# Table casts and splits ahead of the preceding selection's copies in the head, and tile 14's last layer behind tile 15's first, in a gather, interaction and tower kernel

## The reference

```python
e = jnp.stack([tbl_0[ids[:, 0]], ..., tbl_31[ids[:, 31]]], axis=1)
dots = jnp.einsum('bnd,bmd->bnm', e, e)
z = dots[:, iu, ju]
h = jnp.concatenate([z, dense_ctx], axis=1)
h = jnp.maximum(h @ W_top1 + b_top1, 0.0)
h = jnp.maximum(h @ W_top2 + b_top2, 0.0)
y = h @ W_top3
```

## Time and profile before

| what | value |
|---|---|
| median of 3 runs | 585.84 us (584.89 to 585.88) |
| the profiled execution's own time | 583.17 us |
| its span | 581.1 us |
| TensorE matmuls busy | 503.9 us, 87% of the span |
| TensorE weight loads busy | 479.1 us, 82% |
| POOL busy | 419.8 us, 72% |
| VectorE busy | 360.5 us, 62% |
| ScalarE busy | 263.8 us, 45% |
| mean granted clock of TensorE | 0.977 |
| moved by DMA | 70.15 MB, mean 121 GB/s |

### The profile page before, as it was taken

One profiled execution on the slowest core, in us unless ns is written; L12 is line 12 of the kernel. 1 busy time (PEld: TensorE's weight loads), 2 busy tenths in 40 slices (PEclk: granted clock), 3 DMA queues, 4 the chain that ended last, 5 costly groups with the idle time before them and its releaser, 6 DMA issues.

```text
span 581.1 us, 16242 instructions
## 1 busy us (share of the span) xinstructions
PE 503.9 (87%) x7108; PEld 479.1 (82%) x7108; DVE 360.5 (62%) x747; ACT 263.8 (45%) x390; POOL 419.8 (72%) x440
## 2 busy tenths in 40 slices
PE   0266679999999999999999999999999999997786
PEld 0266679898989989898989899898989898996685
DVE  1334467676757577658667677657767675754543
ACT  0223255454546255444636345544645445533542
POOL 6777777777777777777777777777777777777710
PEclk9997799999999999999999999999999999998799
DMA  5999434444433444434443443444443443433310
GB/s 132 257 253 241 108 98 116 115 118 122 117 116 105 127 115 116 119 111 127 115 115 111 120 120 113 115 119 121 118 117 106 133 117 105 119 102 109 105 35 0
DMA packets 35595, 70.15 MB, mean 121 GB/s; under 512 B 13107, under 2 KB 18627, under 8 KB 35527
## 3 DMA queue, kind: packets, MB, share of 16 engines
q0 software_dynamic: 20832, 56.91, 35.1%
q1 hardware_dynamic: 14695, 12.22, 8.9%
HBM read 69.09 MB, written 0.01 MB: 119 GB/s over the span
## 4 chain that ended last, share of the span: by engine, by line
PE 40%; POOL 35%; issue 12%; DVE 5%; ACT 4%; DMA 2%; POOLq 0%; DVEq 0%
POOL rows L318 35%; PE sel_ps L416 15%; PE gram_ps L356 9%; PE tr_ps L332 7%; PE gram_ps L378 4%; DMA rows<-in_tbl,ids_sb 2%; PE gram_ps L388 2%; DVE sel_low L614 2%; ACT sel_high L769 1%; DVE onehot L631 1%; ACT emb_t L537 1%; DVE emb_t L537 1%; ACT emb_t L545 1%; PE gram_ps L396 1%; PE sel_ps L356 1%
## 5 line engine op out<-in xcount | busy, mean ns | idle before, releaser
L318 POOL DMA_INDIRECT rows<-in_tbl,ids_sb x434 | 419.1, 966 | 134.4 <-issue 129.8
L416 PE MATMUL sel_ps<-onehot,sel_high 125*128 125x256 f32 x624 | 164.6, 301 | 24.8 <-DVE sel_low L614 22.6
L537 ACT COPY emb_t<-tr_ps 128x512 f32<-128x512 f32 (+1 forms) x112 | 124.3, 1114 | 100.9 <-PE tr_ps L332 99.9
L416 PE MATMUL sel_ps<-onehot,sel_low 125*128 125x256 f32 x624 | 158.8, 291 | 0.0
L416 PEld LDWEIGHTS sel_ps<-onehot,sel_high 125*128 125x128 f32 x624 | 124.9, 200 | 30.4 <-DVE sel_low L614 23.8
L332 PE MATMUL tr_ps<-ident,rows 128*128 128x128 f32 x868 | 117.5, 279 | 33.2 <-DMA rows<-in_tbl,ids_sb 25.6
L537 DVE COPY emb_t<-tr_ps 128x512 f32<-128x512 f32 (+1 forms) x112 | 120.4, 1086 | 29.0 <-PE tr_ps L332 28.1
L332 PEld LDWEIGHTS tr_ps<-ident,rows 128*128 128x128 f32 x868 | 98.4, 143 | 38.7 <-issue 29.4
L356 PEld LDWEIGHTS gram_ps<-emb_t 128*64 128x64 f32 x3840 | 116.9, 139 | 15.3 <-issue 12.0
L356 PE MATMUL gram_ps<-emb_t 128*64 128x62 f32 x3840 | 121.8, 224 | 8.4 <-ACT emb_t L537 5.6
L416 PEld LDWEIGHTS sel_ps<-onehot,sel_low 125*128 125x128 f32 x624 | 125.1, 200 | 0.0
(11 more groups left out here) (48 smaller groups left out, 157.6 us busy)
## 6 DMA issues: line engine op xcount, KB each, us to landing
rows<-in_tbl,ids_sb POOLq DMA_INDIRECT x434
sel_raw<-in_tbl SPq DMA_DIRECT2D x5, 896.0 KB
sel_ids<-in_ids_by_field SPq DMA_DIRECT2D x35, 128.0 KB
w_sb<-in_W_top SPq DMA_DIRECT2D x1, 1024.0 KB, 22.8
sel_raw<-in_tbl SPq DMA_DIRECT2D x5, 104.0 KB
dots_t<-in_ids_by_field SPq DMA_DIRECT2D x4, 128.0 KB, 5.8
w_sb<-in_W_top SPq DMA_DIRECT2D x1, 512.0 KB, 27.0
ids_sb<-in_ids SPq DMA_DIRECT2D x1, 240.0 KB, 3.1
```

Source lines behind the costliest of these rows:

```text
L318: pool.indirect_dma_start(out=rows[:, slot, :], out_offset=None, in_=tables[f], in_offset=bass.IndirectOffsetOnAxis(ap=ids_sb[:, t, f:f + ...
L416: last = nc.tensor.matmul(sel_ps[j % 2][:, h, :], table[:, i, c, h * P:(h + 1) * P], onehot[:, c, :], start=(c == 0 and table is sel_high) ...
L537: copy(emb_t[t % PAIR][:, h, :, at[0]:at[-1] + 1].rearrange("p (g s) f -> p f s g", s=QUAD), tr_ps[h][g % 2][:, 0:len(at), :].rearrange("p ...
```

## The change

Three things change.

In the head, ScalarE casts the first two tables ahead of the first selection's copies, and each later table one place sooner than before. VectorE's splits move in the same way: splits 0 and 1 stand together behind quad 1, split 2 behind quad 2, split 3 behind quad 4, split 4 behind quad 5. The one-hots keep their places. TensorE's order in the head is the same.

In the tail, TensorE runs tile 14's layer 3 behind tile 15's layer 1 instead of ahead of tile 15's turn. VectorE runs tile 15's turn copy ahead of tile 14's layer 2 relu, and tile 14's y copy behind tile 15's layer 1 relu. ScalarE's order in the tail is the same.

The third part is bookkeeping: the number of gathered selected fields becomes a list with one entry for each pair of tiles, (1, 0, 0, 0, 0, 0, 0, 0), and the helpers that count jobs are written for such a list. The wait of a selection for its table is now asked for by every selection of pair 0 and by every selection of table 0, instead of by every selection of pairs 0 and 1.

```diff
-GATHERED_FIRST = 1
+GATHERED = (1, 0, 0, 0, 0, 0, 0, 0)
...
-        return n_rows + (GATHERED_FIRST if t < PAIR else 0)
+        return n_rows + GATHERED[t // PAIR]
...
-        p, at = (t + 1) // PAIR, range(0, EARLY) if t % PAIR else range(EARLY, n_sel)
-        if t == 0:
-            at = range(GATHERED_FIRST, n_sel)
-        return [(p, i) for i in at] if p < tiles // PAIR else []
+        p = (t + 1) // PAIR
+        if p >= tiles // PAIR:
+            return []
+        own = [(p, i) for i in range(GATHERED[p], n_sel)]
+        return own if t == 0 else own[:EARLY] if t % PAIR else own[EARLY:]
...
-                    if p < 2:
-                        pe.wait_ge(tables_split, (i - GATHERED_FIRST) % n_sel + 1)
+                    if i < GATHERED[0] or p == 0:
+                        pe.wait_ge(tables_split, table_place(i) + 1)
...
                 layer2(t - 1)
-                layer3(t - 1)
                 turn(t)
                 layer1(t)
+                layer3(t - 1)
                 layer2(t)
                 layer3(t)
...
                 turn_dots(t)
+                turn_copy(dve, 0, copy, t)
                 layer2_copy(dve, 0, bias_relu, t - 1)
+                layer1_copy(dve, 0, bias_relu, t)
                 y_copy(t - 1)
-                turn_copy(dve, 0, copy, t)
-                layer1_copy(dve, 0, bias_relu, t)
                 layer2_copy(dve, 0, bias_relu, t)
                 y_copy(t)
...
-            for g in range(quads):
-                emb_copy(dve, 0, copy, g)
-                if g in SELECT_AFTER:
-                    split_table(SELECT_AFTER.index(g))
-                    job = next(next_jobs)
-                    for half in range(2):
-                        build_onehot(job, half)
-            for n in range(n_sel - GATHERED_FIRST, n_sel):
-                split_table(n)
+            emb_copy(dve, 0, copy, 0)
+            emb_copy(dve, 0, copy, 1)
+            split_table(0)
+            split_table(1)
+            for half in range(2):
+                build_onehot(first_jobs[1], half)
+            emb_copy(dve, 0, copy, 2)
+            split_table(2)
+            for half in range(2):
+                build_onehot(first_jobs[2], half)
+            emb_copy(dve, 0, copy, 3)
+            emb_copy(dve, 0, copy, 4)
+            split_table(3)
+            for half in range(2):
+                build_onehot(first_jobs[3], half)
+            emb_copy(dve, 0, copy, 5)
+            split_table(4)
+            for half in range(2):
+                build_onehot(first_jobs[4], half)
+            emb_copy(dve, 0, copy, 6)
...
-            for g in range(quads):
-                emb_copy(act, 1, copy, g)
-                if g in SELECT_AFTER:
-                    high_table(SELECT_AFTER.index(g))
-                    copy_selected(0, next(first_jobs))
-            for n in range(n_sel - GATHERED_FIRST, n_sel):
-                high_table(n)
+            emb_copy(act, 1, copy, 0)
+            emb_copy(act, 1, copy, 1)
+            high_table(0)
+            high_table(1)
+            copy_selected(0, first_jobs[0])
+            emb_copy(act, 1, copy, 2)
+            high_table(2)
+            copy_selected(0, first_jobs[1])
+            emb_copy(act, 1, copy, 3)
+            emb_copy(act, 1, copy, 4)
+            high_table(3)
+            copy_selected(0, first_jobs[2])
+            emb_copy(act, 1, copy, 5)
+            high_table(4)
+            copy_selected(0, first_jobs[3])
+            emb_copy(act, 1, copy, 6)
```

More of the change, by code:

```diff
@@ L78, in n_gathered @@
     def n_gathered(t):
-        return n_rows + (GATHERED_FIRST if t < PAIR else 0)
+        return n_rows + GATHERED[t // PAIR]
     rows_before = [sum(n_gathered(i) for i in range(t)) for t in range(tiles)]
-    assert n_gathered(0) <= quads * QUAD
+    assert len(GATHERED) == tiles // PAIR and max(GATHERED) == GATHERED[0] <= quads * QUAD - n_rows
     def places(t, k):
@@ L103, in jobs, with table_place @@
     def jobs(t):
-        p, at = (t + 1) // PAIR, range(0, EARLY) if t % PAIR else range(EARLY, n_sel)
-        if t == 0:
-            at = range(GATHERED_FIRST, n_sel)
-        return [(p, i) for i in at] if p < tiles // PAIR else []
+        p = (t + 1) // PAIR
[3 more added lines that the diff above has]
+        return own if t == 0 else own[:EARLY] if t % PAIR else own[EARLY:]
+    jobs_before = [sum(n_sel - GATHERED[q] for q in range(p)) for p in range(tiles // PAIR + 1)]
     def job_number(p, i):
-        return p * n_sel + i - GATHERED_FIRST
+        return jobs_before[p] + i - GATHERED[p]
     def ids_loads(p, i):
-        first, j = n_sel - GATHERED_FIRST, job_number(p, i)
-        return len(range(j % 2 + (first if (first - j) % 2 == 0 else first + 1) - j % 2, j + 1, 2))
+        j = job_number(p, i)
+        return len([n for n in range(jobs_before[1], j + 1) if n % 2 == j % 2])
     def jobs_in_bank(bank, p):
-        return len(range(bank, (p + 1) * n_sel - GATHERED_FIRST, 2))
-    turns_odd, turns_even = quads - 1, quads + 1
+        return len(range(bank, jobs_before[p + 1], 2))
+    def table_place(i):
+        return (i - GATHERED[0]) % n_sel
     def quad_turned(t, at):
@@ L194, in ids_of @@
         def ids_of(p, i):
-            return first_ids[:, i - GATHERED_FIRST, :] if p == 0 else sel_ids[job_number(p, i) % 2][:]
+            return first_ids[:, i - GATHERED[0], :] if p == 0 else sel_ids[job_number(p, i) % 2][:]
         onehot = sbuf("onehot", [select_rows, SELECT_CHUNKS, pair_cols], f32r)
@@ L278, in _ @@
                 load_sel_ids(*job)
-            for n in range(GATHERED_FIRST, n_sel):
-                load_table(n)
-            for n in range(GATHERED_FIRST):
+            for n in sorted(range(n_sel), key=table_place):
                 load_table(n)
@@ L516, in _ @@
             pe.wait_ge(ident_ready, 1)
-            first_jobs = iter(jobs(0))
+            first_jobs = jobs(0)
             for g in range(quads):
@@ L521, in _ @@
                 if g in SELECT_AFTER:
-                    job = next(first_jobs)
                     for h in range(D_HALVES):
-                        select(job, h)
+                        select(first_jobs[SELECT_AFTER.index(g)], h)
             for t in range(1, last_tile, PAIR):
@@ L610, in split_table @@
             def split_table(at):
-                n = (at + GATHERED_FIRST) % n_sel
+                n = (at + GATHERED[0]) % n_sel
                 dve.wait_ge(tables_high, at + 1)
@@ L731, in last_periods @@
                 turn_dots(t)
+                turn_copy(dve, 0, copy, t)
                 layer2_copy(dve, 0, bias_relu, t - 1)
+                layer1_copy(dve, 0, bias_relu, t)
                 y_copy(t - 1)
-                turn_copy(dve, 0, copy, t)
-                layer1_copy(dve, 0, bias_relu, t)
                 layer2_copy(dve, 0, bias_relu, t)
                 y_copy(t)
-            first_jobs = jobs(0)
-            next_jobs = iter(first_jobs[1:] + jobs(1)[:1])
+            first_jobs = jobs(0) + jobs(1)[:1]
             for half in range(2):
                 build_onehot(first_jobs[0], half)
-            for g in range(quads):
-                emb_copy(dve, 0, copy, g)
-                if g in SELECT_AFTER:
-                    split_table(SELECT_AFTER.index(g))
-                    job = next(next_jobs)
-                    for half in range(2):
-                        build_onehot(job, half)
-            for n in range(n_sel - GATHERED_FIRST, n_sel):
-                split_table(n)
+            emb_copy(dve, 0, copy, 0)
[18 more added lines that the diff above has]
+            emb_copy(dve, 0, copy, 6)
+            for at in range(5, n_sel):
+                split_table(at)
             dve.wait_ge(weights_loaded, 5 * DMA)
@@ L856, in last_periods @@
                 layer2_copy(act, 1, bias_relu, t)
-            first_jobs = iter(jobs(0))
-            for g in range(quads):
-                emb_copy(act, 1, copy, g)
-                if g in SELECT_AFTER:
-                    high_table(SELECT_AFTER.index(g))
-                    copy_selected(0, next(first_jobs))
-            for n in range(n_sel - GATHERED_FIRST, n_sel):
-                high_table(n)
+            first_jobs = jobs(0)
+            emb_copy(act, 1, copy, 0)
[14 more added lines that the diff above has]
+            emb_copy(act, 1, copy, 6)
+            for at in range(5, n_sel):
+                high_table(at)
             act.wait_ge(weights_loaded, 5 * DMA)
```

## The result

The changed kernel took 583.16 us (median of 20 runs) against 584.98 of the kernel before in the same comparison: ratio 0.9969, 95% interval 0.9956 to 0.9981, so 1.8 us or 0.31% faster. Its profiled execution took 582.69 us, with a span of 580.7 against 581.1. The profiled pair thus differ by 0.4 us only, less than the medians; what went into the 0.4 can be read from the two traces.

A forecast was written before the change was run, and what follows sets the result against it. The prediction took POOL's single queue of gathers to bound the kernel. Ring wait -1.0, splits +0.5 and tail -0.9 summed to -1.4, so 584.4 us against the median 585.84, range 582.3 to 586.1.

The forecast's parts named there:

- the prediction's last line: Forecast wrong if last gather moves over 2 us, clock after it falls below 1.00, or last layer 2's gap grows.
- What bounds the kernel: Whole run: POOL's 434 gathers, about 1.25 us each, 542 of 581 us; TensorE's savings elsewhere become waits for rows.
- Rival 4: TensorE is the bound after all: the head's 9 to 11 us come through, about 575 us; chance 0.03.
- Ring wait: Head, gather at 82.03: POOL's extra wait for transposes with the ring full disappears, -1.0 us.
- Splits: Head: five VectorE splits still hold gathers, at other places; +0.5 us, between -0.1 and +1.1.
- rival 1: Head: two back-to-back splits hold a gather as one; sum -0.8, 585.0 us, no change that can be told; chance 0.30.
- the rule: Head: a gather beginning inside or just ahead of a split is held to its end, then needs 0.82 us.
- Tail: After the last pack copies: tile 15's turn starts 0.89 us sooner, layer 3 covered; -0.9 us, between -0.3 and -0.9.
- Rival 3: Last 256 gram matmuls: earlier waits for rows lower TensorE's clock, costing 3.1 us, 587.5; chance 0.07.
- Rival 2: Head: timed runs lose more at the ring than the profiled one, up to 1.4 + 2.7, about 582.5 us; chance 0.20.
- The first gram: TensorE's head: starts at 64 to 66 instead of 74.90, winning 9 to 11 us on TensorE.
- the last gather's end: End of POOL's queue: the prediction put the last gather at 554 to 555.

The follow-up runs named there:

- the early ids: Split from PSUM plus idle tail transposes, with SP loading the next pair's first two selections' ids ahead of the weights: 574.10 us, ratio 0.9822 to the kernel before.
- the tail alone: Only the change's new tail order, with the head of the kernel before: ratio 0.9983 (0.9966 to 1.0001) to that kernel.
- the split from PSUM: Changed kernel with the full VectorE split reading the rounded table from PSUM, written there by ScalarE in four pieces: 575.75 us, ratio 0.9836 to the kernel before.

## Why the prediction was right

The forecast was 584.4 against 585.84, a fall of 1.4 us; measured were 1.8 (583.16 against 584.98). Sign and size were right, and 583.16 lies in the range. Part of the agreement in size is luck. In the profiled execution the terms were -1.0 - 0.6 - 0.9 = -2.5, and the clock gave back 1.63 that the sum did not hold: two misses that cancel in part. By the prediction's last line a granted clock below 1.00 behind the last gather would make the forecast wrong. It was seen in that execution and not in the later one of the same kernel, and the median came out all the same.

- **What bounds the kernel.** Right. TensorE's 11 us of the head turned into waits for rows, 9.7 us more in the changed kernel, and again, 5.2 more, with the early ids. Rival 4 (TensorE is the bound) fell.
- **Ring wait, -1.0.** Right: the 1.31 us wait stands in both profiles with the old head and in none with the new head and the splits unchanged.
- **Splits, +0.5 between -0.1 and +1.1.** The one step that failed. The prediction placed the first pair "back to back from 26.55 to 31.1". The second table landed too late for that: its cast waited 1.69 us for the load, a wait that the prediction left out. The pair cost 1.57 + 1.08 = 2.65 us instead of 3.1 or 4.3; the last three cost the 4.7 that were forecast. The profiled term was 7.4 - 8.0 = -0.6, below the term's whole range. (That range also leaves out the 0.1 between its own 4.7 and 4.8.) What a joined pair does was settled against rival 1 by the run that joins it: a gather slips in between. That the splits hold the gathers, and the 0.82 behind each, was right, and taking the hold away proved worth more than the whole change. One part of the rule was not: no gather that began just ahead of a split was held, down to 0.12 us ahead. The held sum moves from execution to execution: 6.6 to 9.1 us over the profiles with the new head and all splits kept, against 8.0 and 7.6 in the two with the old head. No single one of them says more than that the term is near 0.
- **Tail, -0.9.** Right on the path: 0.90 from the packs to layer 1, layer 3 covered. In the timed runs the tail alone is not clear of no change.
- **Rival 3 (the clock).** Not as described. The clock fell, but in layer 1, where it cost 1.63 us, and not in the last gram, which ran at 1.00. The tail-alone kernel, whose head is the old one, shows the same fall, so it does not take the earlier waits for rows. It did not turn the sign in the timed runs.
- **Rival 2 (more loss at the ring in the timed runs).** Not borne out. The kernel before had medians of 585.0 to 586.2 in the four comparisons and single runs down to 583.2, so its one profile lies at the low end of an ordinary spread. The tail-alone profile took 585.91 us, 2.74 more than that one, with the same 1.31 at the ring; its first 90 us hold the same 69 gathers and 68.0 us of POOL, so its longer time lies behind the head. (The 582.5 of this rival is not its sum either: 585.84 - 1.4 - 2.7 = 581.7, below the stated range.)
- **The first gram** was at 63.85 and the last gather's end at 553.6, both just ahead of the 64 to 66 and 554 to 555 that were named.

## What to carry to other kernels

Where one queue issues without a break for nearly the whole span, look for its rare long instructions before anything else: here five of 434 gathers lost 8 us, and freeing them gave 6 to 8 us at the end, while 11 us won on TensorE gave 1.0. Here it paid to give the VectorE instruction that read two inputs from SBUF beside such gathers one of them from PSUM, though that cost four more copies for each table. And a saving of 1 us at the end of a kernel can be given back by TensorE's clock in one execution and not in the next, so read several profiles before naming a cause.

## What was not expected

Most of a gather can run beside a split: one that began 0.12 us ahead of a split, and one 0.04 behind a split's start, ran their usual 0.94 or 0.95; each one begun 0.13 to 1.3 behind it waited to the split's end, and then needed 0.82 more (0.90 once, with the next split following without a gap). No split ran longer for it: all took 2.28 to 2.31. Two splits without a gap let one gather through between them. The Trainium skill, "SBUF — State Buffer", section "Who interferes with whom", says that an instruction with two SBUF inputs contends with a GpSimd instruction that reads SBUF; the split from PSUM bears that out (no gather held, and 10 us less than the kernel before). Its remark that a tensor_tensor doesn't stall descriptor generation does not hold for these gathers.
